# Feed-forward part of a transformer layer: norm applications on ScalarE, attention halves on GpSimd, TensorE's branch ahead of the last value matmul

## The chip, the cores and the metric

The kernel runs on one core of a Trainium2 chip. The core's engines are TensorE (PE: matmuls; PEld: its weight loads), VectorE (DVE), ScalarE (ACT), GpSimd (POOL) and SyncE (SP), which issues the DMAs. Each has its own instruction stream, worked through in program order, and they wait for each other on semaphores. Time is the device time of one execution in microseconds (us).

## The reference

One transformer layer on 4 sequences of 1024 tokens with 256 features, in float32: attention with 16 query heads and 4 key/value heads of width 16, then a gated feed-forward part of width 1024 with integer weights, each with a residual and a layer norm behind it.

```python
def _layernorm(x, axis=-1, eps=1e-05):
    m = jnp.mean(x, axis=axis, keepdims=True)
    v = jnp.var(x, axis=axis, keepdims=True)
    return (x - m) / jnp.sqrt(v + eps)
...
        q = q * cos + _rotate_half(q) * sin
        k = k * cos + _rotate_half(k) * sin
...
        scores = jnp.einsum('bqkgd,bskd->bkgqs', qg, k) * scale
        attn = jax.nn.softmax(scores, axis=-1)
        out = jnp.einsum('bkgqs,bskd->bqkgd', attn, v).reshape(B, S, E)
        return out @ wo
...
        Wg = _dequant(gate_w, gate_scale)   # (w - 128) * scale
        g = jnp.einsum('bsh,ih->bsi', hidden_state, Wg)
        u = jnp.einsum('bsh,ih->bsi', hidden_state, Wu)
        h = jax.nn.silu(g) * u
        return jnp.einsum('bsi,hi->bsh', h, Wd)
...
    x = _layernorm(x + _L0_attn_ref(...), axis=-1)
    x = _layernorm(x + _L0_ffn_ref(...), axis=-1)
```

## The kernel before

The kernel has three parts in time. The projections come first. Then attention runs over 8 pairs of key/value heads, 4 halves for each pair, 8 key tiles `t` for each half. The feed-forward part comes last, over 8 blocks `m` of 512 tokens, from about 768 us of the trace to its end. The change touches the last half of attention and everything behind it.

Matmul operands that need more than the fast format holds are split in two: a high part (`_h`, a cast) and a low part (`_l`, the rest). So nearly every tensor that TensorE reads costs a copy and a subtraction on other engines.

A block `m` of the feed-forward part is this, with `it` from 0 to 7 over slices of 128 of the 1024 hidden features:

- TensorE: `gate_up(it)`, 8 matmuls of 128x512 (L1071), into one of two `pair_bank`s; from `it` 2 on, `down(it-2)`, 8 matmuls of 128x256 (L1080), into `pv_bank` and a ring bank. After `down(3)` come the transposes of the next block's `x1` (L995). After `down(5)` comes the output projection `project_out` of the block after that (24 matmuls, L987), then `down(6)` and `down(7)`.
- ScalarE: `silu(it)` (L893), and behind it, in this order, the high part `hid_h(it-1)` of the hidden slice before (L883). The high part of the transposed `x1` (L847) comes at `it` 5.
- VectorE: `hid(it)` (L758), and between two of them a piece of the work around the block: `y` of the block before (L715, L720), the residual of the next block (L682), its norm statistics (L662, L668, L670), its norm application to `x1` (L675, at `it` 4), the high and low parts of the attention output for the block after that (`bring_attn`: L704, L707, at `it` 4), the second norm of the block before (statistics at `it` 5, application to `y`, also L675, at `it` 7), and the low part of `x1T` (L697, at `it` 5).
- GpSimd: `hid_l(it)` (L528), which `down(it)` waits for, and the two reciprocal square roots (L513, behind `hid_l(2)` and `hid_l(5)`). In block 0 it also scales the last pair's attention output (L509, behind `hid_l(4)`).

So each hidden slice goes PE, ACT, DVE, ACT, POOL and back to PE. The order on each engine is written out by hand. `hid` and `silu` have two buffers each.

TensorE's feed-forward code exists twice, with and without the low parts of the weights. A flag computed from the weights (`use_low`) chooses the copy; TensorE loads it and branches. Before the change this happens right in front of `gate_up(0)` of block 0, behind the last value matmul `pv` (L971) and `project_out(1)`. With these inputs the copy without low parts runs.

## Time and profile before

| what | us |
|---|---|
| median of 3 runs | 1015.37 (1012.94 to 1015.94) |
| the profiled execution, its own time | 1014.48 |
| its span, first to last instruction | 1012.7 |
| TensorE busy | 947.9 |
| VectorE busy | 822.5 |
| ScalarE busy | 696.4 |
| GpSimd busy | 237.3 |

The mean granted clock of TensorE over the span is 0.957 of full speed. In the page's 40 slices of 25.3 us each, the last ten belong to the feed-forward part: TensorE is at 8 or 9 tenths in most of them, VectorE at 6 to 8, ScalarE at 3 or 4 and GpSimd at 2 to 5. A row of the timeline gives the start in us, the duration in us (of all merged instructions together, where it ends in x2 or x4), the engine, the line, the operation, what it writes and reads, and in brackets how long the engine sat idle before it and whom it waited for. Starts and ends of different engines in one trace can be compared.

### The profile page before, as it was taken

The page shows a single profiled execution, that of the slowest core. Times are in us where ns is not written, and L with a number is a line of the kernel's source. Part 1 is how long each engine was busy: PE and PEld are TensorE (multiplying, and loading weights), DVE is VectorE, ACT ScalarE, POOL GpSimd, SP SyncE. Part 2 cuts the span into 40 slices and gives each one's busy share as a digit, 9 for nine tenths or more (in the row PEclk, how much of TensorE's full clock was granted, in tenths as well). Part 3 has the DMA queues.
Part 4 walks back from the last instruction along what each step waited for, and adds up shares of the span by engine and source line. Part 5 has one row for each costly group of instructions (what it writes and reads, how often), then busy time and mean ns, then how long its engine had stood idle before and what let it go on. Part 6 is the DMA issues. An engine that isn't in the chain of part 4 may idle for free.

```text
span 1012.7 us, 15932 instructions
## 1 busy us (share of the span) xinstructions
PE 947.9 (94%) x5632; PEld 475.1 (47%) x5632; DVE 822.5 (81%) x1601; ACT 696.4 (69%) x878; POOL 237.3 (23%) x162
## 2 busy tenths in 40 slices
PE   7886999999999999999999999999997899999985
PEld 3343433333333333333333333333336787777774
DVE  2756689999999999999999999999833678877756
ACT  1324588998999899989989898999983333433332
POOL 9874274000000000000000000000002445544433
PEclk9886589999999999999999999999999999999997
DMA  5667443142232332332323313301201010011001
GB/s 158 207 215 156 146 104 103 33 78 71 52 68 61 73 67 47 83 67 51 79 53 69 68 41 73 87 24 46 73 8 53 21 42 18 25 42 43 22 21 42
DMA packets 48450, 70.65 MB, mean 70 GB/s; under 512 B 15152, under 2 KB 27184, under 8 KB 48368
## 3 DMA queue, kind: packets, MB, share of 16 engines
q1 hardware_dynamic: 47552, 66.45, 26.2%
q0 software_dynamic: 816, 3.15, 1.0%
q8 instruction: 47, 0.77, 0.3%
q14 instruction: 35, 0.29, 0.1%
HBM read 46.47 MB, written 16.25 MB: 62 GB/s over the span
## 4 chain that ended last, share of the span: by engine, by line
PE 66%; DVE 13%; issue 4%; POOL 4%; ACT 4%; POOLq 0%; DVEq 0%; ACTq 0%
PE pv_bank L971 24%; PE ring_bank L948 24%; DVE block_max L607 8%; PE pair_bank L1021 7%; PE pair_bank L1071 6%; POOL hid_l L528 3%; PE pv_bank L1080 2%; ACT probs L867 2%; DVE hid L758 1%; PE ring_bank L1080 1%; DVE x L675 1%; POOL rstd L513 1%; ACT hid_h L883 1%; PE ring_bank L987 1%; ACT silu L893 1%
## 5 line engine op out<-in xcount | busy, mean ns | idle before, releaser
L867 ACT ACTIVATE probs<-pair_bank 128x1024 f32<-128x1024 f32 x512 | 495.6, 1024 | 48.9 <-PE pair_bank L1021 48.9
L607 DVE TENSOR_REDUCE block_max<-ring_bank 128x1 f32<-128x512 f32 x720 | 467.1, 684 | 41.1 <-PE ring_bank L948 30.0
L948 PE MATMUL ring_bank<-k_max,q_sb 64*128 64x512 f32 x1024 | 348.2, 487 | 18.6 <-DMA q_sb<-q_parts 7.8
L948 PEld LDWEIGHTS ring_bank<-k_max,q_sb 64*128 64x128 f32 x1024 | 144.8, 191 | 301.6 <-DVE block_max L607 151.8
L971 PE MATMUL pv_bank<-probs,v_sb 128*32 128x512 f32 x2048 | 273.6, 606 | 1.4 <-ACT probs L867 1.3
L1021 PE MATMUL pair_bank<-q_sb,k_sb 64*128 64x512 f32 x1024 | 251.6, 425 | 1.8 <-ACT probs L867 1.8
L509 POOL TENSOR_TENSOR attn<-attn,inv_rows 128x1024 f32<-128x1024 f32 x8 | 19.5, 2438 | 532.9 <-DMA inv_rows<-inv_d 532.9
L1021 PEld LDWEIGHTS pair_bank<-q_sb,k_sb 64*128 64x128 f32 x1024 | 117.8, 186 | 31.9 <-ACT probs L867 15.7
L893 ACT ACTIVATE silu<-pair_bank,gate_s 128x512 f32<-128x512 f32 x64 | 44.1, 689 | 125.3 <-PE pair_bank L1071 125.2
L528 POOL TENSOR_TENSOR hid_l<-hid,hid_h 128x512 fp32r<-128x512 f32 x64 | 84.7, 1329 | 143.8 <-ACT hid_h L883 143.8
L838 ACT ACTIVATE above<-ring_bank 128x512 f32<-128x512 f32 x152 | 90.6, 598 | 34.5 <-PE ring_bank L948 31.4
L604 DVE CUSTOM_DVE_ANT_0 above<-ring_bank,above 128x512 f32<-128x512 f32 x152 | 103.5, 689 | 12.7 <-ACT above L838 11.3
L758 DVE SCALAR_TENSOR_TENSOR hid<-pair_bank,up_s,silu 128x512 f32<-128x512 f32 x64 | 47.1, 742 | 68.3 <-ACT silu L893 60.1
L971 PEld LDWEIGHTS pv_bank<-probs,v_sb 128*32 128x32 f32 x2048 | 40.3, 108 | 76.0 <-issue 73.3
L811 ACT ACTIVATE high<-rotated 128x512 fp32r<-128x512 f32 (+1 forms) x20 | 12.6, 630 | 64.9 <-POOL rotated L469 64.9
L918 PE MATMUL pair_bank<-x_in,wq_sb 128*128 128x512 f32 x64 | 36.4, 721 | 15.0 <-DMA x_in<-xT 8.2
L1080 PE MATMUL pv_bank<-down_h,hid_h 128*128 128x256 f32 x128 | 37.9, 318 | 12.2 <-POOL hid_l L528 11.5
L1071 PE MATMUL pair_bank<-x1T_h,gate_h 128*128 128x512 f32 x128 | 42.4, 414 | 5.7 <-issue 2.9
L883 ACT ACTIVATE hid_h<-hid 128x512 fp32r<-128x512 f32 x64 | 40.0, 625 | 8.9 <-DVE hid L758 8.7
L1071 PE MATMUL pair_bank<-x1T_l,gate_h 128*128 128x512 f32 x128 | 41.3, 405 | 0.0
L1071 PE MATMUL pair_bank<-x1T_h,up_h 128*128 128x512 f32 x128 | 41.0, 403 | 0.0
L1071 PE MATMUL pair_bank<-x1T_l,up_h 128*128 128x512 f32 x128 | 40.6, 399 | 0.0
(95 smaller groups left out, 879.4 us busy)
## 6 DMA issues: line engine op xcount, KB each, us to landing
q_sb<-q_parts SPq DMA_DIRECT2D x192, 64.0 KB, 2.3
k_max<-k_parts SPq DMA_DIRECT2D x96, 96.0 KB, 3.2
k_sb<-k_parts SPq DMA_DIRECT2D x96, 64.0 KB, 2.4
x_in<-xT SPq DMA_DIRECT2D x8, 512.0 KB, 5.0
q_parts<-high SPq DMA_DIRECT2D x16, 256.0 KB, 4.4
q_parts<-low SPq DMA_DIRECT2D x16, 256.0 KB, 4.7
attn<-pv_sb SPq DMA_DIRECT2D x128, 32.0 KB
inv_rows<-inv_d SPq DMA_DIRECT2D x64, 64.0 KB, 2.3
```

Of the source, the lines that this page charges most:

```text
L528: pool.tensor_tensor(hid_l[:, it, :], hid[it % 2][:], hid_h[:, it, :].bitcast(fp32), ALU.subtract).then_inc(hid_l_ready, 1)
L604: dve.tensor_tensor_reduce(out=buf[:], in0=bank[:], in1=buf[:], scale=1.0, scalar=-3.0e38, op0=ALU.add, op1=ALU.max, accum_out=block_max[h ...
L607: dve.reduce_max(block_max[half % 2][:, col:col + 1], bank[:], axis=AX.X).then_inc(ring_used, 1)
L758: dve.scalar_tensor_tensor(out=hid[it % 2][:], in0=pair_bank[it % 2][:, 1, :], scalar=up_s[:, it:it + 1], in1=silu[it % 2][:], op0=ALU.mul ...
L838: act.activation(above[(count - 1) % 2][:], ring_bank[places[key] % BANKS][:], ACT.Relu).then_inc(above_ready, 1)
L867: act.activation(probs[t % 2][:, 2 * pr:2 * pr + 2, :], pair_bank[pr][:], ACT.Exp, scale=D ** -0.5).then_inc(probs_ready, 1)
L893: act.activation(silu[it % 2][:], pair_bank[it % 2][:, 0, :], ACT.Silu, scale=gate_s[:, it:it + 1]).then_inc(silu_ready, 1)
L948: pe.matmul(bank[:], q_sb[k][rows, i, qt * P:(qt + 1) * P], k_max[k // QH][rows, kind * CH:(kind + 1) * CH], start=True, stop=True).then_i ...
L971: ins = pe.matmul(pv_bank[32 * j:32 * j + 2 * D, :], v_sb[s][:, t, :], probs[t % 2][:, 2 * (j % 2) + j // 2, :], start=(t == 0), stop=(t = ...
L1021: ins = pe.matmul(pair_bank[pr][:, r, :], k_sb[s][rows, t * P:(t + 1) * P], q_sb[k][rows, pr, :], start=True, stop=True)
L1071: ins = pe.matmul(pair_bank[it % 2][:, u, :], w[:, k, it * P:(it + 1) * P], v[c][:, k, :], start=(q == 0), stop=(q == len(terms) - 1))
L1080: ins = pe.matmul(sum_bank[t // 2][:, (t % 2) * E:(t % 2 + 1) * E], v[:, k, t * P:(t + 1) * P], w[:, k, :], start=(k == 0 and t % 2 == 0 a ...
```

## The change

Four things change.

1. Both norm applications go from VectorE to ScalarE. VectorE computed (x - mean) * rstd from two pointers. ScalarE computes rstd * x + offset in one Identity activation. So VectorE also writes `minus_mean` (128x4), and GpSimd multiplies it with rstd into `offset` (128x4) behind each reciprocal square root. For block 0's `x1` ScalarE does it in the last half of attention, behind the exponentials of `t` 3. In the blocks `x1` comes at `it` 4, behind `hid_h(3)`, and `y` at `it` 7, behind `hid_h(6)` and ahead of `hid_h(7)`.
2. `bring_attn` goes from VectorE to GpSimd in two pieces (a cast and a subtraction of 128x512 each), behind `hid_l(0)` and `hid_l(3)`. The halves of blocks 0 and 1 are made early, during attention. The high and low parts of `x1T` move from `it` 5 to `it` 6.
3. TensorE's branch stands ahead of the last `pv`; both copies of its feed-forward code now begin with that `pv` and `project_out(1)`. VectorE computes `use_low` ahead of the low part of `x1T` for block 0. A one-column Silu of a spare tile lets ScalarE load its Silu table ahead of `gate_up(0)`.
4. The space for the early attention halves comes from memory that is used earlier: the weights are split on GpSimd in six pieces of 1024 columns in place of three of 2048, and `pv` reads `v_all` directly, so that the 16 DMAs into `v_sb` and their share of the waits go.

```diff
-                sp.dma_start(v_sb[s][:], v_all[:, 2 * pair + s]).then_inc(kv_loaded[s], 16)
...
+            for n, (w, w_h, w_l) in enumerate(((gate_w, gate_h, gate_l), (up_w, up_h, up_l), (down_w, down_h, down_l))):
                 flat_h, flat_l = (t[:].rearrange("p k n -> p (k n)") for t in (w_h, w_l))
-                pool.tensor_copy(flat_h, w_f[:]).then_inc(w_high, 1)
-                pool.wait_ge(w_high, n + 1)
-                pool.tensor_tensor(flat_l, w_f[:], flat_h.bitcast(fp32), ALU.subtract).then_inc(w_split, 1)
+                rows = w.shape[0] // 2
+                for half in range(2):
+                    i = 2 * n + half
+                    cols = slice(half * I, (half + 1) * I)
...
+            def bring_attn(m, c, k):
+                if m > 1:
+                    pool.wait_ge(wo_ready, 2 * m - 2)
+                src = attn[:, 2 * (m // 2) + k, c * CH:(c + 1) * CH]
+                pool.wait_ge(norm_done, 2 * (m // 2) + 2)
+                pool.tensor_copy(attn_h[c][:, k, :], src).then_inc(attn_h_ready, 1)
+                pool.wait_ge(attn_h_ready, 2 * m + k + 1)
+                pool.tensor_tensor(attn_l[c][:, k, :], src, attn_h[c][:, k, :].bitcast(fp32), ALU.subtract).then_inc(attn_in_ready, 1)
+            def rsqrt(m, ve, r, mm, off, added, done, used, off_done):
+                pool.wait_ge(added, 2 * m + 2)
+                if m:
+                    pool.wait_ge(used, TT * m)
                 pool.tensor_tensor(r[:], ve[:], neg_half[:], ALU.pow).then_inc(done, 1)
+                pool.wait_ge(done, m + 1)
+                pool.tensor_tensor(off[:], mm[:], r[:], ALU.mult).then_inc(off_done, 1)
...
             for pair in range(1, PAIRS - 1):
+                if pair == PAIRS - 2:
+                    for c in range(2):
+                        for k in range(KE):
+                            bring_attn(c, c, k)
                 normalize(pair, False, False)
-            rsqrt(1, var_eps, rstd, eps_added, rstd_ready)
+            rsqrt1(0)
...
                         if it == 2 and not (last and c == 1):
-                            rsqrt(m + 2, var_eps, rstd, eps_added, rstd_ready)
+                            rsqrt1(m + 1)
                         if it == 4 and first and c == 0:
                             normalize(PAIRS - 1, False, True)
+                        if it in (0, 3) and not last:
+                            bring_attn(m + 2, c, it // 3)
                         if it == 5 and not (first and c == 0):
-                            rsqrt(m, var_eps2, rstd2, eps2_added, rstd2_ready)
+                            rsqrt2(m - 1)
             each(B, ffn)
-            rsqrt(2 * B, var_eps2, rstd2, eps2_added, rstd2_ready)
+            rsqrt2(2 * B - 1)
...
                 dve.wait_ge(ready, TT * m + TT)
+                if m:
+                    dve.wait_ge(used, m)
+                dve.tensor_scalar(mm[:], mv[:, :, 0], -1.0, None, ALU.mult).then_inc(added, 1)
                 dve.tensor_scalar(ve[:], mv[:, :, 1], EPS, None, ALU.add).then_inc(added, 1)
-            def apply_norm(m, src, dst, mv, r, ready, done):
-                dve.wait_ge(ready, m + 1)
-                for t in range(TT):
-                    dve.tensor_scalar(dst[:, t, :], src[:, t, :], mv[:, t, 0:1], r[:, t:t + 1], ALU.subtract, ALU.mult).then_inc(done, 1)
...
-                        if it == 4:
-                            if nxt:
-                                if prev:
-                                    dve.wait_ge(sum_ready, m)
-                                norm1_apply(m + 1, 1 - c)
-                            if not last:
-                                bring_attn(b + 1, c)
                         if it == 5:
                             if prev:
                                 norm2_stats(m - 1, 1 - c)
                                 norm2_aggregate(m - 1)
-                            if nxt:
-                                split_x1T(m + 1, 1 - c)
-                        if it == KI - 1 and prev:
-                            norm2_apply(m - 1, 1 - c)
...
+                        if last and k == HALVES - 1 and t == KT - 5:
+                            norm1_apply(0, 0)
...
+            def apply_norm(m, src, dst, r, off, ready, done):
+                act.wait_ge(ready, m + 1)
+                for t in range(TT):
+                    act.activation(dst[:, t, :], src[:, t, :], ACT.Identity, bias=off[:, t:t + 1], scale=r[:, t:t + 1]).then_inc(done, 1)
+            def norm1_apply(m, c):
+                if m > 1:
+                    act.wait_ge(sum_ready, m - 1)
+                apply_norm(m, x_res[c], x1[c], rstd, offset, offset_ready, x1_ready)
+            def norm2_apply(m, c):
+                apply_norm(m, y[c], y[c], rstd2, offset2, offset2_ready, y_ready)
...
+            act.activation(table_carrier[:], neg_half[:, 0:1], ACT.Silu)
...
-                        if it == 5 and not (last and c == 1):
+                        if it == 4 and not (last and c == 1):
+                            norm1_apply(m + 1, 1 - c)
+                        if it == 6 and not (last and c == 1):
                             split_x1T(m + 1, 1 - c)
+                        if it == 7 and not (first and c == 0):
+                            norm2_apply(m - 1, 1 - c)
...
-                    ins = pe.matmul(pv_bank[32 * j:32 * j + 2 * D, :], v_sb[s][:, t, :], probs[t % 2][:, 2 * (j % 2) + j // 2, :],
+                    ins = pe.matmul(pv_bank[32 * j:32 * j + 2 * D, :], v_all[:, head, t, :], probs[t % 2][:, 2 * (j % 2) + j // 2, :],
...
-            pe.wait_ge(probs_ready, 2 * last_g + 2)
-            pv(last_g, HALVES * PAIRS - 1, HALVES - 1, KT - 1, True)
-            project_out(1, 1, False)
-            pe.wait_ge(w_split, 3)
+            pe.wait_ge(w_split, 6)
...
+                pe.wait_ge(probs_ready, 2 * last_g + 2)
+                pv(last_g, HALVES * PAIRS - 1, HALVES - 1, KT - 1, True)
+                project_out(1, 1, False)
                 each(B, ffn)
...
```

TensorE at the branch, before (`use_low` is the flag, `pv_bank` the value matmuls, `ring_bank<-wo_*` is `project_out(1)`, the last row `gate_up(0)`):

```order
L1021 MATMUL pair_bank<-q_sb,k_sb 128x512 x4
L971 MATMUL pv_bank<-probs,v_sb 32x512 x8
L987 MATMUL ring_bank<-wo_h,attn_h 128x256 x2
...
L987 MATMUL ring_bank<-wo_l,attn_h 128x256 x2
L1109 TENSOR_LOAD use_low
L1109 ISA x2
L1110 COMPARE_AND_BRANCH
L1071 MATMUL pair_bank<-x1T_h,gate_h 128x512 x2
```

And after:

```order
L1040 MATMUL pair_bank<-q_sb,k_sb 128x512 x4
L990 MATMUL pv_bank<-probs,v_all 32x512 x4
L1126 TENSOR_LOAD use_low
L1126 ISA x2
L1127 COMPARE_AND_BRANCH
L990 MATMUL pv_bank<-probs,v_all 32x512 x4
L1006 MATMUL ring_bank<-wo_h,attn_h 128x256 x2
...
L1085 MATMUL pair_bank<-x1T_h,gate_h 128x512 x2
```

The load of the flag and the branch moved ahead of the last `pv` and of `project_out(1)`.

ScalarE from `silu(4)` to the end of block 1, before:

```order
L893 ACTIVATE silu<-pair_bank,gate_s 128x512
L883 ACTIVATE hid_h<-hid 128x512
L893 ACTIVATE silu<-pair_bank,gate_s 128x512
L883 ACTIVATE hid_h<-hid 128x512
L847 ACTIVATE x1T_h<-ring_bank 128x512 x2
L893 ACTIVATE silu<-pair_bank,gate_s 128x512
L883 ACTIVATE hid_h<-hid 128x512
L893 ACTIVATE silu<-pair_bank,gate_s 128x512
L883 ACTIVATE hid_h<-hid 128x512 x2
```

And after:

```order
L907 ACTIVATE silu<-pair_bank,gate_s 128x512
L897 ACTIVATE hid_h<-hid 128x512
L878 ACTIVATE x_0<-x_res,offset,rstd 128x256 x4
L907 ACTIVATE silu<-pair_bank,gate_s 128x512
L897 ACTIVATE hid_h<-hid 128x512
L907 ACTIVATE silu<-pair_bank,gate_s 128x512
L897 ACTIVATE hid_h<-hid 128x512
L845 ACTIVATE x1T_h<-ring_bank 128x512 x2
L907 ACTIVATE silu<-pair_bank,gate_s 128x512
L897 ACTIVATE hid_h<-hid 128x512
L878 ACTIVATE v_all<-v_all,offset,rstd 128x256 x4
L897 ACTIVATE hid_h<-hid 128x512
```

Two groups of four 128x256 activations are new; the second (`y`, which lies in `v_all`) stands between `hid_h(6)` and `hid_h(7)`.

GpSimd up to `hid_l(5)` of block 1, before (the first row is `hid_l` 5 to 7 of block 0 and 0 to 2 of block 1):

```order
L528 TENSOR_TENSOR hid_l<-hid,hid_h 128x512 x6
L513 TENSOR_TENSOR rstd<-var_eps,neg_half 128x4
L528 TENSOR_TENSOR hid_l<-hid,hid_h 128x512 x3
```

And after (the first row is `hid_l` 5 to 7 of block 0 and 0 of block 1):

```order
L556 TENSOR_TENSOR hid_l<-hid,hid_h 128x512 x4
L521 CAST attn_h<-attn 128x512
L523 TENSOR_TENSOR attn_l<-attn,attn_h 128x512
L556 TENSOR_TENSOR hid_l<-hid,hid_h 128x512 x2
L529 TENSOR_TENSOR rstd<-var_eps,neg_half 128x4
L531 TENSOR_TENSOR offset<-minus_mean,rstd 128x4
L556 TENSOR_TENSOR hid_l<-hid,hid_h 128x512
L521 CAST attn_h<-attn 128x512
L523 TENSOR_TENSOR attn_l<-attn,attn_h 128x512
L556 TENSOR_TENSOR hid_l<-hid,hid_h 128x512 x2
```

Two casts, two subtractions and the product for `offset` now stand between the `hid_l` that `down` waits for.

## Rows read from the trace of the kernel before

**Rows 1.** Timeline of TensorE (and its weight loads) from the last value matmul.

```profile
760.82 1.06 PE L971 MATMUL pv_bank<-probs,v_sb 128*32 128x512 f32 x8 [1.31 <-ACT probs L867]
...
767.86 0.83 PE L1071 MATMUL pair_bank<-x1T_h,gate_h 128*128 128x512 f32 x2 [2.91 <-issue]
...
791.96 0.99 PE L1071 MATMUL pair_bank<-x1T_h,gate_h 128*128 128x512 f32 x2 [2.01 <-DVE hid L758]
...
800.26 0.28 PE L1080 MATMUL pv_bank<-down_h,hid_h 128*128 128x256 f32 x1
...
865.83 0.36 PE L1080 MATMUL pv_bank<-down_h,hid_h 128*128 128x256 f32 x1 [1.00 <-POOL hid_l L528]
...
868.70 0.28 PE L1080 MATMUL pv_bank<-down_h,hid_h 128*128 128x256 f32 x1
...
874.87 0.38 PE L1080 MATMUL pv_bank<-down_h,hid_h 128*128 128x256 f32 x1 [0.22 <-POOL hid_l L528]
...
887.02 0.19 PEld L1080 LDWEIGHTS pv_bank<-down_h,hid_h 128*128 128x128 f32 x1 [0.28 <-POOL hid_l L528]
...
944.93 0.19 PEld L1080 LDWEIGHTS pv_bank<-down_h,hid_h 128*128 128x128 f32 x1 [0.28 <-POOL hid_l L528]
...
972.67 0.19 PEld L1080 LDWEIGHTS pv_bank<-down_h,hid_h 128*128 128x128 f32 x1 [0.28 <-POOL hid_l L528]
...
1000.57 0.29 PEld L1080 LDWEIGHTS pv_bank<-down_h,hid_h 128*128 128x128 f32 x1 [0.29 <-POOL hid_l L528]
```

**Rows 2.** A 2-us stretch: PE, PEld, DVE, ACT, POOL busy, granted clock, DMA.

```profile
768.00:770.00 2.00, 2.00 (x6) 1.56 (x7) 0.00 (x0) 0.00 (x0) 0.00 (x0) 0.59 0.12 25
```

**Rows 3.** Timeline of VectorE, in block 0 (786.73) and block 3.

```profile
786.73 4.51 DVE L707 TENSOR_TENSOR attn_l<-attn,attn_h 128x512 fp32r<-128x512 f32 x2
...
870.71 0.86 DVE L670 TENSOR_SCALAR var_eps<-mean_var 128x4 f32<-128x4 f32 x1
871.48 1.21 DVE L720 TENSOR_TENSOR v_all<-v_all,x 128x1024 f32<-128x1024 f32 x1
...
873.67 2.27 DVE L675 TENSOR_SCALAR x<-x_res,mean_var,rstd 128x256 f32<-128x256 f32 x4 [0.31 <-POOL rstd L513]
...
884.12 3.32 DVE L675 TENSOR_SCALAR v_all<-v_all,mean_var,rstd 128x256 f32<-128x256 f32 x4
```

**Rows 4.** Timeline of GpSimd in block 3.

```profile
864.41 1.28 POOL L528 TENSOR_TENSOR hid_l<-hid,hid_h 128x512 fp32r<-128x512 f32 x1 [6.36 <-ACT hid_h L883]
...
871.65 1.91 POOL L513 TENSOR_TENSOR rstd<-var_eps,neg_half 128x4 f32<-128x4 f32 x1
873.53 1.29 POOL L528 TENSOR_TENSOR hid_l<-hid,hid_h 128x512 fp32r<-128x512 f32 x1
...
884.35 2.62 POOL L528 TENSOR_TENSOR hid_l<-hid,hid_h 128x512 fp32r<-128x512 f32 x2 [1.57 <-ACT hid_h L883]
```

**Rows 5.** Timeline of ScalarE, last half of attention, first table load, block 3.

```profile
749.20 3.77 ACT L867 ACTIVATE probs<-pair_bank 128x1024 f32<-128x1024 f32 x4 [0.19 <-PE pair_bank L1021]
...
771.34 1.28 ACT L893 ACT_TABLE_LOAD   x1 [8.79 <-PE pair_bank L1071]
...
883.57 1.29 ACT L883 ACTIVATE hid_h<-hid 128x512 fp32r<-128x512 f32 x2 [1.13 <-DVE hid L758]
```

**Rows 6.** Groups by line and shape: count, then busy us, mean ns, idle before.

```profile
L893 ACT ACTIVATE silu<-pair_bank,gate_s 128x512 f32<-128x512 f32 x64 | 44.1, 689 | 125.3 <-PE pair_bank L1071 125.2
L847 ACT ACTIVATE x1T_h<-ring_bank 128x512 fp32r<-128x512 f32 x16 | 8.7, 598 | 5.0 <-PE ring_bank L995 5.0
...
L818 ACT ACTIVATE v_all<-ring_bank 128x256 f32<-128x256 f32 x4 | 1.5, 366 | 0.0
```

**Rows 7.** The same, GpSimd.

```profile
L513 POOL TENSOR_TENSOR rstd<-var_eps,neg_half 128x4 f32<-128x4 f32 x16 | 21.6, 1350 | 35.7 <-DVE var_eps L670 34.5
...
L500 POOL CAST gate_h<-w_f 128x2048 fp32r<-128x2048 f32 x1 | 1.9, 1891 | 0.1
```

**Rows 8.** Timeline of the tail.

```profile
1007.88 1.38 DVE L675 TENSOR_SCALAR v_all<-v_all,mean_var,rstd 128x256 f32<-128x256 f32 x4 [1.12 <-POOL rstd L513]
```

More of the change, by code:

```diff
@@ L109, in layer @@
         rstd = sb("rstd", [P, TT])
+        minus_mean, offset = sb("minus_mean", [P, TT]), sb("offset", [P, TT])
         attn_l = [sb(f"attn_l{c}", [P, KE, CH], f32r) for c in range(2)]
         two = ExitStack()
-        w_raw = sb("w_raw", [P, KE * I], i32, two)
-        w_f = sb("w_f", [P, KE * I], fp32, two)
+        w_raw = sb("w_raw", [P, I], i32, two)
+        w_f = sb("w_f", [P, I], fp32, two)
+        above = [sb(f"above{c}", [P, CH], fp32, two) for c in range(2)]
+        k_max = [sb(f"k_max{s}", [P, S + CH], f32r, two) for s in range(UNITS)]
         q_sb = [sb(f"q_sb{k}", [P, G // GROUPS, CH], f32r, two) for k in range(HALVES)]
-        k_max = [sb(f"k_max{s}", [P, S + CH], f32r, two) for s in range(UNITS)]
         k_sb = [sb(f"k_sb{s}", [P, S], f32r, two) for s in range(UNITS)]
-        v_sb = [sb(f"v_sb{s}", [P, KT, 2 * D], fp32, two) for s in range(UNITS)]
-        above = [sb(f"above{c}", [P, CH], fp32, two) for c in range(2)]
         probs = [sb(f"probs{c}", [P, G, CH], fp32, two) for c in range(2)]
@@ L795, in _ @@
             norm2_aggregate(2 * B - 1)
-            norm2_apply(2 * B - 1, 1)
         @block.scalar
```

66 lines of the change are left out of this document (30 added, 36 removed).

## Prediction

> **What bounds the kernel now.** I looked first at the 40 slices of the page: the feed-forward part is where the change lies, and TensorE is at 8 or 9 tenths there. TensorE sets the pace, so every other engine counts only where TensorE waits for it. Then I read TensorE's timeline for the rows with idle time in front [rows 1]. The blocks follow each other evenly: the last `down(7)` of block 0 starts at 800.26, that of block 5 at 944.93, so blocks 1 to 5 take 28.93 us each. In block 3 TensorE stands still for 1.00 us ahead of `down(0)` (865.83) and for shorter times ahead of `down(3)` (874.87) and `down(7)` (887.02); `down(1)` at 868.70 waits for nothing. All of these waits end with `hid_l` on GpSimd [rows 1]. `down(it)` needs the chain `silu(it+1)`, `hid_h(it)`, `hid_l(it)` behind `gate_up(it+1)`: 0.6 us until `hid_h`, 0.62, and 1.28, with the semaphores about 2.8 us. `down` and `gate_up` of one `it` take 2.87 us together (865.83 to 868.70) [rows 1, 4 to 6]. So the chain just fits, and a microsecond put into it on ScalarE or GpSimd comes out on TensorE.
>
> Three places cost more. In front of `gate_up(0)` of block 0 stands a gap of 2.91 us that the profile gives to nobody (the branch), and the clock behind it is 0.59 [rows 1, 2]. The Silu table is loaded only at 771.34, when the first `silu` is wanted [rows 5]. In block 0 VectorE needs 4.51 us for two subtractions that lie beside GpSimd's work and makes TensorE wait 2.01 us at 791.96 [rows 1, 3].
>
> **Attention.** Without the `v_sb` DMAs nothing ends earlier that TensorE waits for; I count nothing. The six weight pieces on GpSimd have 500 us until they are wanted. The early attention halves lie there too, with nothing behind them that is due.
>
> **The norm application as a price.** The trace has no Identity with two pointers. From below it is bounded by the 128x256 copy out of PSUM, 0.366 us, from above by the 128x512 `silu` with one pointer, 0.689 [rows 6]. One pointer costs 0.689 - 0.598 = 0.09 (`silu` against the copy `x1T_h`, both from PSUM), so two make 0.55 of the copy's 0.366. Two `hid_h` in a row take 1.29, where groups of small ones from PSUM overlap by about 0.1, so I take 0.48 each in a row, 2.0 us for four (bounds 1.5 and 2.8). The Trainium skill (ScalarE: Activation LUTs, What ACT_TABLE_LOAD costs) prices an activation with pointers at 186 ns plus 0.833 ns a column plus 93 ns for each pointer, less 93 ns where they follow each other; that gives an estimate of 0.49 each, and the sum would stay as it is.
>
> **The boundary.** ScalarE runs the exponentials of the last half without a pause: four take 3.77 us from 749.20 [rows 5]. The application for block 0 goes between them, so everything behind comes 2.0 us later. VectorE did it for free. The last value matmuls ran at 760.82, after a gap of 1.31 us, so the `pv` before had ended at 759.5 [rows 1]. Now that end is at 761.5, the branch follows, and with the same gap (2.9 to 3.2 us) the last `pv` starts at about 764.7, 3.9 us later. From there to `gate_up(0)` it was 7.04 us (760.82 to 767.86), of which 3.2 were the branch. That leaves 3.8, plus 1.8 if the half clock that followed the gap now falls on `pv` and `project_out`: `gate_up(0)` starts at 770.3, 2.4 us later than before. Then block 0 runs at full clock from its start. Block 0 took 32.4 us to its `down(7)` (767.86 to 800.26). Out of these go 1.7 for the half clock, 0.8 for the table load (1.28, of which 0.5 was covered by `gate_up(1)`), 2.0 for VectorE and 1.6 for the half clock that I expect behind it, as behind the gap of 2.91. In come 1.1 on GpSimd, where the last pair's scaling now stands behind two added operations and makes `hid_l(5)` late. 27.4 us remain, and `down(7)` of block 0 starts at 797.7: **-2.6 us** (bounds: -4.4 if the clock holds through the new gap, 0 if ScalarE's four applications open a second gap that halves the clock inside attention).
>
> **Blocks 1 to 5, walked in block 3.**
> - `hid_l(0)` ends at 865.69 [rows 4]. The cast takes 1.89/4 = 0.47 [rows 7], the subtraction 1.28 like `hid_l`, with waits 1.9 together. `hid_l(1)` ends at 868.9 and `down(1)` starts at 869.0 instead of 868.70: 0.3 late.
> - At `it` 3 `var_eps` lasted 0.86 us because `hid_l(2)` was running beside it, and the power 1.91 because the 1.21 us of L720 were [rows 3, 4]; alone it is 0.87. So operations of the two engines on SBUF exclude each other in these rows. `minus_mean` adds 0.1 ahead of L720. The product for `offset` is bounded by 0.01 (its share of a 1.28-us subtraction by size) and 0.87 (the power, same shape); I take 0.2, since it is a subtraction's kind of work and not a power. `hid_l(3)` starts at 873.9 instead of 873.53, `down(3)` at 875.3 instead of 874.87: 0.4 late, which takes in the first 0.3.
> - ScalarE applies the norm from 874.0 to 876.0; the transposes want it at 876.2. It just fits. The second attention piece (1.9) and `hid_l(4)` (1.3) fit under `down(3)`, transposes and `gate_up(6)`.
> - VectorE's part is gone: 2.27 + 3.32 and the attention halves. It bought little, since TensorE's waits in these blocks end with GpSimd, and the one on `hid_h` (1.13 us of ScalarE at 883.57, from 882.44) lay beside `project_out`.
> - At the end `silu(7)` comes 0.4 later, `hid_h(6)` follows at once (882.8 to 883.4), then `y` until 885.4, then `hid_h(7)` until 886.0 and `hid_l(7)` until 887.45. `down(7)` starts at 887.5 instead of 887.02.
>
> That is +0.45 a block, **+2.3 us** for five (bounds -1.5 and +8).
>
> The Trainium skill (GPSIMD Reference, section 4.1, Engine selection) says to keep two-input elementwise work on VectorE, since GpSimd takes about twice as long. The rows agree (1.28 us for 512 columns on GpSimd, 1.21 for 1024 in L720 on VectorE). By the rule the move would lose its 1.3 us a block; by the walk above only 0.3 of them reach TensorE, because the rest lies under its matmuls.
>
> **Blocks 6 and 7.** They have no `project_out`, so nothing covers `hid_h(7)` behind `y`. Before, `hid_h(7)` followed `hid_h(6)`, and `down(7)` started at 972.67 and 1000.57 [rows 1]. Now 2.0 us of `y` lie between, of which GpSimd's `hid_l(6)` hides 0.6: +1.4 in each, and +0.2 from `down(3)` in block 6: **+3.0 us**.
>
> **The tail.** Behind the last `down` come the second norm and its application, once 1.38 us on VectorE [rows 8], now 2.0 on ScalarE, with `minus_mean` 0.1 and `offset` 0.3 ahead: **+1.0 us**.
>
> Sum: -2.6 + 2.3 + 3.0 + 1.0 = +3.7. The profiled execution took 1014.48 (its span of 1012.7 and 1.8 around it), so 1018.2 for the like of it; the median of the runs lies 0.9 higher, and I give 1019.0.
>
> **Rivals.**
> - *The cover is larger than I think* (faster). The clock holds at the branch (-1.8), and the blocks get shorter by 0.3 instead of longer, because GpSimd no longer shares SBUF with 8 us of VectorE's work a block, so that `hid` and `hid_l` come earlier (-0.75 x 5 = -3.8 against my sum), and so in block 6 (-0.5). 3.7 - 6.1 = -2.4 to -4: 1012. For it speaks that VectorE is busy in 6 to 8 tenths there and its rows are stretched (2.27, 3.32) [rows 3]; against it that TensorE's waits end elsewhere.
> - *GpSimd's small operations are dear* (slower, much). If the product costs what the power costs, it delays `hid_l(3)` by 0.7 more, and the chain repeats it at `it` 5: +1.4 x 6, +0.7 in the tail, about +9: 1028. For it: no small operation of GpSimd other than the power is timed in this part. It decides from a product of 0.4 us on.
> - *Gain and loss cancel* (no change). An application costs 0.38 in place of 0.48: 0.4 less in each `y`, -0.2 x 5 for the blocks, -0.8 for blocks 6 and 7, -0.4 in the tail: +1.5, 1017.
> - *The change doesn't do what it says*, the gap of the branch is not covered: that is in my sum already (the gap begins 1.3 us earlier in its half and costs the same).
>
> **How the numbers follow.** My forecast, slower by 2 to 6 us: 0.45. Cancelling: 0.25. Faster rival: 0.18. Dear small operations: 0.12. A measurement of this kernel tells 0.3% (3 us) from no change. The forecast case lies above that bound in about 0.37 of its 0.45; so slower 0.37 + 0.12 = 0.49, same 0.33, faster 0.18. The range from 1011.5 to 1025 leaves out the dear rival and the edge of the faster one, 0.18 together; around the likeliest alone it would be 1016.5 to 1022.
>
> **What would show it.** A row of four 128x256 activations of about 2.0 us at `it` 4 and 7; a `hid_h(7)` that starts when `y` ends, and a `down(7)` that waits for `hid_l`; `down(1)` with a wait of 0.3; a last `pv` at about 764.7 and `gate_up(0)` at 770 with full clock; VectorE busy less by about 8 us a block with no shorter block. Wrong would be a period of blocks 1 to 5 below 28.9, a `gate_up(0)` before 768, or applications below 0.4 us.

## The result and the profile after

The changed kernel took 1018.82 us (median of 5 runs, 1016.94 to 1020.36), the kernel before 1013.04 in the runs beside it (5 runs, 1011.89 to 1015.94): a ratio of 1.0047, 95% interval [1.0029, 1.0065], so slower by 0.3 to 0.65%. The profiled execution took 1019.23, its span 1017.4 (before: 1014.48 and 1012.7). VectorE's busy time fell from 822.5 to 761.0 us, ScalarE's rose from 696.4 to 725.2, GpSimd's from 237.3 to 269.4, TensorE's stayed (947.7). In all, 61 us less work on VectorE bought nothing.

I cut the span at the start of `project_out(0)` (741.63 before, 741.14 after) and at the first matmul of each `down(7)`. The numbers are differences of such rows of the two timelines.

| stretch | before | after | difference | forecast |
|---|---|---|---|---|
| start to `project_out(0)` | 741.63 | 741.14 | -0.5 | 0 |
| from there to `down(7)` of block 0 | 58.63 | 57.95 | -0.7 | -2.6 |
| blocks 1 to 5 | 144.67 | 145.90 | +1.2 | +2.3 |
| blocks 6 and 7 | 55.64 | 59.27 | +3.6 | +3.0 |
| from the last `down(7)` to the end | 12.13 | 13.14 | +1.0 | +1.0 |
| sum | | | +4.7 | +3.7 |

TensorE's timeline after, for the rows that answer to [rows 1] (start, duration, engine, line, operation, idle time before and its releaser):

```profile
753.55 0.56 PE L1040 MATMUL pair_bank<-q_sb,k_sb 64*128 64x512 f32 x2 [1.36 <-ACT probs L865]
...
766.31 1.06 PE L990 MATMUL pv_bank<-probs,v_all 128*32 128x512 f32 x8 [3.03 <-issue]
771.78 0.63 PE L1085 MATMUL pair_bank<-x1T_h,gate_h 128*128 128x512 f32 x2
...
799.09 0.28 PE L1094 MATMUL pv_bank<-down_h,hid_h 128*128 128x256 f32 x1
...
865.20 0.36 PE L1094 MATMUL pv_bank<-down_h,hid_h 128*128 128x256 f32 x1 [0.98 <-POOL hid_l L556]
868.27 0.19 PEld L1094 LDWEIGHTS pv_bank<-down_h,hid_h 128*128 128x128 f32 x1 [0.46 <-POOL hid_l L556]
874.59 0.39 PE L1094 MATMUL pv_bank<-down_h,hid_h 128*128 128x256 f32 x1 [0.40 <-POOL hid_l L556]
886.59 0.19 PEld L1094 LDWEIGHTS pv_bank<-down_h,hid_h 128*128 128x128 f32 x1 [0.47 <-POOL hid_l L556]
...
944.99 0.39 PE L1094 MATMUL pv_bank<-down_h,hid_h 128*128 128x256 f32 x1 [0.26 <-POOL hid_l L556]
...
974.48 0.58 PE L1094 MATMUL pv_bank<-down_h,hid_h 128*128 128x256 f32 x1 [0.66 <-POOL hid_l L556]
...
1001.78 0.39 PE L1094 MATMUL pv_bank<-down_h,hid_h 128*128 128x256 f32 x1 [1.76 <-POOL hid_l L556]
1004.26 0.58 PE L1094 MATMUL pv_bank<-down_h,hid_h 128*128 128x256 f32 x1 [1.26 <-POOL hid_l L556]
```

The waits of before stand at the same places with the same releaser; those at `down(7)` of blocks 6 and 7 (974.48, 1004.26) have grown. Two are new: 1.36 us at 753.55, inside attention, behind ScalarE's four applications, and that of the weight load of `down(1)` for `hid_l`, 0.46 us at 868.27, which the forecast named. The wait of 2.01 us in block 0 (791.96) is gone. The gap of the branch is as long as before (3.03, 2.91), only ahead of `pv`.

ScalarE's timeline after, at the boundary, at the end of block 3 and at the end of the kernel [rows 5, 8]:

```profile
750.53 2.06 ACT L878 ACTIVATE x<-x_res,offset,rstd 128x256 f32<-128x256 f32 x4
...
768.05 1.28 ACT L893 ACT_TABLE_LOAD   x1
...
881.99 0.62 ACT L897 ACTIVATE hid_h<-hid 128x512 fp32r<-128x512 f32 x1
882.51 2.08 ACT L878 ACTIVATE v_all<-v_all,offset,rstd 128x256 f32<-128x256 f32 x4
884.50 0.61 ACT L897 ACTIVATE hid_h<-hid 128x512 fp32r<-128x512 f32 x1
...
1011.92 2.07 ACT L878 ACTIVATE v_all<-v_all,offset,rstd 128x256 f32<-128x256 f32 x4 [9.12 <-POOL offset L531]
```

Four applications take 2.06 to 2.08 us. `hid_h(7)` stands behind `y` and starts when it ends. GpSimd in block 3 [rows 4]:

```profile
864.99 0.61 POOL L521 CAST attn_h<-attn 128x512 fp32r<-128x512 f32 x1
865.68 1.29 POOL L523 TENSOR_TENSOR attn_l<-attn,attn_h 128x512 fp32r<-128x512 f32 x1
...
871.10 1.91 POOL L529 TENSOR_TENSOR rstd<-var_eps,neg_half 128x4 f32<-128x4 f32 x1 [0.17 <-DVE var_eps L703]
873.10 0.20 POOL L531 TENSOR_TENSOR offset<-minus_mean,rstd 128x4 f32<-128x4 f32 x1
873.25 1.29 POOL L556 TENSOR_TENSOR hid_l<-hid,hid_h 128x512 fp32r<-128x512 f32 x1
```

The product for `offset` takes 0.20 us, and the power is as long as before, though VectorE has less to do. The granted clock in 2-us stretches of the boundary (the third number from the end; first the stretch, its length and the busy time of PE, PEld, DVE, ACT, POOL), answering to [rows 2]:

```profile
752.00:754.00 2.00, 0.64 (x6) 0.19 (x2) 0.00 (x0) 2.00 (x4) 0.00 (x0) 0.96 0.00 0
754.00:756.00 2.00, 1.65 (x8) 0.49 (x10) 0.00 (x0) 2.00 (x3) 0.00 (x0) 0.50 0.00 0
...
758.00:760.00 2.00, 2.00 (x9) 1.12 (x7) 0.00 (x0) 0.21 (x1) 0.00 (x0) 0.50 0.00 0
760.00:762.00 2.00, 2.00 (x14) 0.57 (x12) 0.00 (x0) 2.00 (x3) 0.00 (x0) 0.83 0.00 0
...
768.00:770.00 2.00, 2.00 (x11) 2.00 (x11) 0.00 (x0) 1.52 (x3) 0.00 (x0) 0.50 0.12 26
```

The clock is at 0.50 of full (1.2 of 2.4 GHz) twice: for 6.8 us behind the 1.36-us gap (753.9 to 760.7), and again for 3.4 us behind the branch.

### The profile page after: what moved, and what is told of

Its sections match the earlier page's. It is cut to its first block, busy times and chain, and to the rows that moved or that the text cites. A ratio compares the mean times of both kernels' runs of the same rounds, so it can differ in the third digit from the quotient of the medians.

```text
span 1017.4 us, 16003 instructions
## 1 busy us (share of the span) xinstructions
PE 947.7 (93%) x5632; PEld 475.4 (47%) x5632; DVE 761.0 (75%) x1521; ACT 725.2 (71%) x943; POOL 269.4 (26%) x222
## 4 chain that ended last, share of the span: by engine, by line
PE 69%; DVE 9%; ACT 6%; POOL 4%; issue 2%; POOLq 0%; ACTq 0%; DVEq 0%
PE pv_bank L990 24%; PE ring_bank L967 24%; PE pair_bank L1085 8%; DVE block_max L637 8%; PE pair_bank L1040 7%; POOL hid_l L556 3%; PE pv_bank L1094 2%; PE ring_bank L1094 2%; ACT probs L865 2%; ACT v_all L878 1%; POOL rstd L529 1%; ACT hid_h L897 1%; PE ring_bank L1006 1%; ACT silu L907 1%; PE ring_bank L1014 1%
## 5 line engine op out<-in xcount | busy, mean ns | idle before, releaser
L865 ACT ACTIVATE probs<-pair_bank 128x1024 f32<-128x1024 f32 x512 | 495.7, 1024 | 51.0 <-PE pair_bank L1040 51.0
L990 PE MATMUL pv_bank<-probs,v_all 128*32 128x512 f32 x2048 | 274.7, 609 | 3.1 <-issue 3.0
L556 POOL TENSOR_TENSOR hid_l<-hid,hid_h 128x512 fp32r<-128x512 f32 x64 | 82.3, 1287 | 124.2 <-ACT hid_h L897 117.4
L990 PEld LDWEIGHTS pv_bank<-probs,v_all 128*32 128x32 f32 x2048 | 40.4, 108 | 78.1 <-issue 77.6
```

The costliest lines, as they stand in the source:

```text
L556: pool.tensor_tensor(hid_l[:, it, :], hid[it % 2][:], hid_h[:, it, :].bitcast(fp32), ALU.subtract).then_inc(hid_l_ready, 1)
L865: act.activation(probs[t % 2][:, 2 * pr:2 * pr + 2, :], pair_bank[pr][:], ACT.Exp, scale=D ** -0.5).then_inc(probs_ready, 1)
L990: ins = pe.matmul(pv_bank[32 * j:32 * j + 2 * D, :], v_all[:, head, t, :], probs[t % 2][:, 2 * (j % 2) + j // 2, :], start=(t == 0), stop= ...
```

## The experiments

All runs are compared with runs of the kernel before on the same chip (medians 1011.74, 1012.06 and 1011.87 us). Ratios are to it, in brackets the 95% interval; 0.001 is 1 us. What a single trace adds is read at the cuts above. Between two traces the time from `project_out(0)` to `down(7)` of block 0 moves by 2 to 3 us through the clock alone, so the blocks are read singly.

| kernel | ratio | `project_out(0)` to `down(7)` of block 0 | mean of blocks 1 to 5 | block 6 | block 7 | tail |
|---|---|---|---|---|---|---|
| before | 1 | 58.63 | 28.93 | 27.74 | 27.90 | 12.13 |
| after | 1.0047 | 57.95 | 29.18 | 29.49 | 29.78 | 13.14 |
| after again | 1.0052 [1.0037, 1.0067] | 55.55 | 29.19 | 29.46 | 29.22 | 13.15 |
| x1 on VectorE | 1.0047 [1.0030, 1.0064] | 54.72 | 29.20 | 29.44 | 29.82 | 13.12 |
| x1 in two parts | 1.0044 [1.0028, 1.0061] | 54.56 | 29.19 | 29.45 | 29.15 | 13.14 |
| branch back | 1.0053 [1.0032, 1.0073] | 54.95 | 29.20 | 29.46 | 27.70 | 12.58 |
| branch alone | 1.0018 [1.0009, 1.0027] | 58.79 | 28.94 | 27.71 | 26.32 | 11.53 |
| y last | 1.0008 [0.9994, 1.0022] | 56.66 | 28.69 | 28.13 | 26.76 | 12.99 |
| halves on VectorE | 1.0070 [1.0058, 1.0083] | 55.37 | 29.41 | 29.19 | 29.13 | 13.11 |
| hid_h first | 0.9901 [0.9886, 0.9916] | 54.53 | 27.12 | 27.40 | 27.47 | 13.04 |
| hid_h first, before | 0.9908 [0.9893, 0.9923] | 55.77 | 28.14 | 26.81 | 24.75 | 11.50 |
| all three | 0.9832 [0.9819, 0.9845] | 53.41 | 26.97 | 26.29 | 24.90 | 12.60 |
| all three, branch back | 0.9845 [0.9830, 0.9860] | 52.70 | 26.97 | 26.30 | 26.43 | 12.61 |
| and tail on VectorE | 0.9830 [0.9813, 0.9847] | 53.31 | 26.97 | 26.29 | 24.89 | 11.62 |

### The boundary

**x1 of block 0 on VectorE.** Off ScalarE's last half of attention, as before the change:

```diff
-                        if last and k == HALVES - 1 and t == KT - 5:
-                            norm1_apply(0, 0)
...
+            dve.wait_ge(rstd_ready, 1)
+            for t in range(TT):
+                dve.tensor_scalar(x1[0][:, t, :], x_res[0][:, t, :], mean_var[:, t, 0:1], rstd[:, t:t + 1], ALU.subtract, ALU.mult).then_inc(x1_ready, 1)
             split_x1T(0, 0)
```

> The changed kernel, with block 0's norm application (x1) back on VectorE; all other applications stay on ScalarE. Theory: in the changed kernel the four activations in the last half of attention cost their own 2.06 us on ScalarE and, through the gap of 1.36 us that they open in front of the scores of t 5, a stretch of half clock worth another 2 to 2.5 us. So gate_up(0) starts 4 to 4.5 us earlier than in the changed kernel (at about 767.5 in place of 771.78), no row between 750 and 760 shows a clock of 0.50, and the median is about 1014.5 (1018.8 less 4.3). Rival: the half clock comes from something else (the transposes or the branch) and only the 2.06 us come back: 1016.8.

Neither size came. The ratio is that of the changed kernel; the 0.8 us by which its boundary is shorter in the traces (54.72 against 55.55 in "after again") is less than the ratios can tell.

**x1 in two parts.** Two applications at `t` 3 and two at `t` 4:

```diff
-                            norm1_apply(0, 0)
+                            act.wait_ge(offset_ready, 1)
+                        if last and k == HALVES - 1 and t in (KT - 5, KT - 4):
+                            for u in (0, 1) if t == KT - 5 else (2, 3):
+                                act.activation(x1[0][:, u, :], ...)
```

> The changed kernel, with block 0's four applications on ScalarE in two pieces: two behind the exponentials of t 3, two behind those of t 4. The same work on the same engine. Theory: TensorE's one gap of 1.36 us becomes two of about 0.6, the clock stays at full through attention, and gate_up(0) starts 2 to 2.5 us earlier than 771.78: about 1016.5. Rival: the half clock follows from the sum of the idle time or from the transposes: no difference, 1018.8.

The gap of 1.36 fell to 0.38 and 0.41, with no gain that the runs can tell: the rival.

**After again.** No edit.

> The changed kernel once more, unchanged, on the chip of these runs. Theory: the half clock behind the 1.36 us gap of the last half of attention (754 to 760 in its first trace), and that in block 7, are not fixed by the program: the gap and the work behind it will be the same, and the clock behind it full, gate_up(0) 27.3 to 29.4 us behind the start of project_out(0) instead of 30.6. Rival: the gap of 1.36 us halves the clock each time, as its first trace had it (30.6).

The theory held. The rows of the second trace of the same program:

```profile
753.26 0.50 PE L1040 MATMUL pair_bank<-q_sb,k_sb 64*128 64x512 f32 x2 [1.36 <-ACT probs L865]
...
763.62 1.48 PE L990 MATMUL pv_bank<-probs,v_all 128*32 128x512 f32 x8 [2.98 <-issue]
```

and its clock:

```profile
754.00:756.00 2.00, 1.82 (x14) 0.75 (x15) 0.00 (x0) 1.95 (x3) 0.00 (x0) 1.00 0.00 0
756.00:758.00 2.00, 2.00 (x19) 0.91 (x17) 0.00 (x0) 0.84 (x1) 0.00 (x0) 1.00 0.00 0
```

The gap is the same, and the clock behind it is full. It was full too, at the same gap, in "branch back", "y last", "halves on VectorE" and "hid_h first". So the half clock inside attention was that one execution's. In this trace the last `pv` starts 22.77 us behind `project_out(0)`; with x1 on VectorE it is 20.78. The applications do delay it by 2.0, as forecast, but `gate_up(0)` follows only 0.9 later (28.25 and 27.39), because from its start `pv` and what follows ran at half clock for 3.4 us in the one and for 5.9 in the other.

**Branch back** (the changed kernel) and **branch alone** (the kernel before). The first moves the last `pv` and `project_out(1)` ahead of the load of the flag again; the second does the opposite to the kernel before, with `use_low` computed early:

```diff
-            pe.wait_ge(probs_ready, 2 * last_g + 2)
-            pv(last_g, HALVES * PAIRS - 1, HALVES - 1, KT - 1, True)
-            project_out(1, 1, False)
...
+                pe.wait_ge(probs_ready, 2 * last_g + 2)
+                pv(last_g, HALVES * PAIRS - 1, HALVES - 1, KT - 1, True)
+                project_out(1, 1, False)
                 each(B, ffn)
```

> The changed kernel, with TensorE's branch where it was before: behind the last value matmul and project_out(1). Theory: the gap of the branch (3.03 us) is the same length at either place, but ahead of the last value matmul 1.3 us of it lie under ScalarE's last exponentials, and the half clock behind it falls on small matmuls instead of gate_up(0). The step is worth 1 to 2 us: 1020.3. Rival: the branch ahead of pv is worth nothing or costs (its half clock is the same in length): 1018.8 or below.

> The kernel before the change, with one part of the change alone: the flag's load and the branch ahead of the last value matmul (and use_low ahead of the low part of x1T). Theory: the branch costs its 2.9 us wherever it stands, and the 1.31 us that TensorE waited for probs in front of the last pv is hidden under it, so the stretch from project_out(0) to gate_up(0) gets shorter by about 1 us, and block 0 keeps its 32.4 us less what half clock there is behind the gap: 0 to -2 us against the kernel before, ratio 0.998 to 1.000. Rival: the branch is the cause of the whole half clock at the boundary and block 0's clock is worth what I counted (-1.7): -3 us or more, ratio 0.997 or below.

Branch back: no difference, the rival. In its trace the gap of the branch is 2.31 us and the clock behind it stays full. Branch alone: both expectations fell, it is 1.8 us slower. With the branch ahead the gap was 3.29 and `pv`, `project_out` and the first matmuls ran at half clock from 766 to 772; before, the gap was 2.91 behind 1.31 us of waiting. What `pv` no longer waits, the clock takes back: 58.79 against 58.63 us in these two traces. That explains why nothing was gained, and not the 1.8 us: this trace is longer by 3.4 us in its first 61 us, ahead of everything that the edit touches. Where the 1.8 us stand is open.

### The blocks

**y last.** The second norm's application behind `hid_h(7)`:

```diff
-                        if it == 7 and not (first and c == 0):
-                            norm2_apply(m - 1, 1 - c)
                     hid_high(KI * m + KI - 1, KI - 1)
+                    if not (first and c == 0):
+                        norm2_apply(m - 1, 1 - c)
```

> The changed kernel, with the application to y behind hid_h(7) in place of ahead of it. Theory: y delays hid_h(7) by 2.06 us, which blocks 6 and 7 pay nearly in full (29.49 and 29.78 us in the changed kernel, 27.74 and 27.90 before) and blocks 1 to 5 by some tenths. So blocks 6 and 7 fall to about 27.9 each, blocks 1 to 5 to about 29.0, together -4.5 us: 1014.3. Rival: down(7) then waits for something nearly as late (GpSimd's queue, the power for the second norm), or y comes too late for the output and the next block: -1 us or nothing, 1018.

The theory held: 3.9 us by the ratios. Each of blocks 1 to 5 is 0.5 shorter and block 6 1.36. Of the 3.0 in block 7 about 2 are clock, since "branch back", with `y` ahead of `hid_h(7)` but no half clock there, takes 27.70. That this comes and goes for the same code is seen in the kernel before and in "branch alone" behind the same wait for `hid_l` (1.57 and 1.55 us in block 6), one row of each:

```profile
974.00:976.00 2.00, 2.00 (x7) 1.61 (x7) 0.00 (x0) 0.00 (x0) 0.00 (x0) 0.50 0.78 262
```

```profile
978.00:980.00 2.00, 2.00 (x10) 1.63 (x9) 0.00 (x0) 0.25 (x1) 0.00 (x0) 1.00 0.77 262
```

Their blocks 7 take 27.90 and 26.32 us.

Blocks 1 to 5 are now 0.24 shorter than in the kernel before (28.69 against 28.93), so the work taken off VectorE was worth something. In block 3, `down(7)` follows `down(6)` after 0.96 us without a wait, where it was 1.29 (28.68 - 27.72 and 28.92 - 27.63 in the table below). Before, ScalarE waited 1.13 us for `hid` ahead of `hid_h(6)` [rows 5]; now it waits 0.29, ahead of `hid_h(7)`, and `hid_l(6)` starts 0.7 us earlier in the block:

```profile
881.39 0.63 ACT L897 ACTIVATE hid_h<-hid 128x512 fp32r<-128x512 f32 x1 [0.29 <-DVE hid L766]
```

**Halves on VectorE.** In the blocks `bring_attn` goes back to VectorE at `it` 4:

```diff
-                        if it in (0, 3) and not last:
-                            bring_attn(m + 2, c, it // 3)
...
+                        if it == 4 and not last:
+                            bring_attn(b + 1, c)
```

> The changed kernel with the blocks' attention halves back on VectorE at it 4 (those of blocks 0 and 1 still made early). Theory, from the walk of block 3: GpSimd's pieces cost 0.3 us a block at down(1), and VectorE has room without the norm applications, so blocks 1 to 5 come down from 29.2 to about 28.9 us (-1.5 in all); in block 0 the two subtractions lie beside the scaling of the last pair again and TensorE waits there up to 2 us. In all -1.5 to +0.5 us against the changed kernel, ratio to before 1.003 to 1.005. Rival: taking the halves off VectorE is what kept the blocks as short as they are: blocks 1 to 5 at 29.5 us or more, ratio 1.007 or above.

The theory fell, the rival's sign is right: 29.41 a block against 29.18, 2.3 parts in a thousand slower in all. The starts in block 3, in us behind `down(7)` of block 2, each read from one row of the timeline:

| start of | before | after | halves on VectorE | y last | hid_h first | hid_h first, before |
|---|---|---|---|---|---|---|
| `down(0)` | 7.73 | 7.81 | 7.82 | 7.70 | 6.92 | 6.88 |
| `down(1)` | 10.60 | 10.88 | 10.71 | 10.79 | 10.01 | 9.74 |
| `down(3)` | 16.77 | 17.20 | 17.44 | 17.11 | 15.75 | 15.33 |
| transposes | 17.89 | 18.25 | 18.50 | 18.16 | 16.70 | 17.34 |
| `down(6)` | 27.63 | 27.82 | 28.08 | 27.72 | 26.11 | 26.74 |
| `down(7)` | 28.92 | 29.20 | 29.44 | 28.68 | 27.13 | 28.11 |

GpSimd's first piece costs 0.17 at `down(1)`, of the 0.3 in the walk. But VectorE's halves cost more at `down(3)`:

```profile
869.21 2.08 POOL L529 TENSOR_TENSOR rstd<-var_eps,neg_half 128x4 f32<-128x4 f32 x1 [0.17 <-DVE var_eps L701]
...
870.84 0.75 DVE L727 CAST attn_h<-attn 128x512 fp32r<-128x512 f32 x2
871.37 0.27 POOL L531 TENSOR_TENSOR offset<-minus_mean,rstd 128x4 f32<-128x4 f32 x1
871.60 1.27 POOL L556 TENSOR_TENSOR hid_l<-hid,hid_h 128x512 fp32r<-128x512 f32 x1
```

With VectorE's cast beside them, the power takes 2.08 in place of 1.91 and the product 0.27 in place of 0.20, and both stand ahead of `hid_l(3)`. The kernel before had no such meeting: there the halves stood behind the norm application, which waited for the power [rows 3]:

```profile
875.86 0.75 DVE L704 CAST attn_h<-attn 128x512 fp32r<-128x512 f32 x2
```

So this run prices halves on VectorE right behind `hid(3)`. Halves on VectorE that wait for the power as before were not run with the norm on ScalarE.

**hid_h first.** ScalarE makes `hid_h(it-1)` ahead of `silu(it)` and no longer behind it; once in the changed kernel, once in the kernel before:

```diff
                         n = KI * m + it
+                        if it:
+                            hid_high(n - 1, it - 1)
                         act.wait_ge(gu_ready, n + 1)
...
-                        if it:
-                            hid_high(n - 1, it - 1)
-                        elif not (first and c == 0):
+                        if it == 0 and not (first and c == 0):
                             act.wait_ge(down_ready, 2 * m)
```

> The changed kernel with one order on ScalarE changed: hid_h(it-1) is issued ahead of silu(it) and no longer behind it. Theory: every wait of down on hid_l in the blocks (0.98 at down(0), 0.46 at down(1), 0.84 at down(3), 0.5 at down(7)) is length of the chain silu, hid_h, hid_l behind gate_up, and hid_h has to wait 0.69 us for a silu that it doesn't need; ahead of it, hid_h comes about 2 us earlier: blocks 1 to 5 come down from 29.2 to 27.0 to 27.7 us, in all -10 to -14 us against the changed kernel, ratio to before 0.991 to 0.995. The wait at down(7) behind y stays. Rival: GpSimd's own work (hid_l, the attention pieces, the power) sets these waits; then only the part of hid_h goes, -0.3 us a block or nothing, ratio 1.002 to 1.005.

> The kernel before the change with the one order on ScalarE changed: hid_h(it-1) ahead of silu(it). Theory: the waits of TensorE in the blocks came from the order on ScalarE and have nothing to do with the change, so the kernel before gains as much by it as the changed one did (which went from 1.0047 to 0.9901 of the kernel before, 14.8 us), and since y stands on VectorE and keeps hid_h(7) free, nothing is left over at down(7): ratio 0.984 to 0.988, blocks of 27.0 us. Rival: VectorE, which has 8 us more work in each block, then sets the pace (hid late behind the attention halves and the norm at it 4), and the blocks stay at 28 us: ratio 0.990 to 0.994, and the change is what makes the order pay.

In the changed kernel the theory held, with a little more than its 10 to 14 us: 14.8 us less, blocks of 27.12, and no wait ahead of a matmul in TensorE's rows of block 3. ScalarE's rows there:

```profile
862.86 0.64 ACT L897 ACTIVATE hid_h<-hid 128x512 fp32r<-128x512 f32 x1 [0.82 <-DVE hid L766]
864.48 0.69 ACT L909 ACTIVATE silu<-pair_bank,gate_s 128x512 f32<-128x512 f32 x1 [0.98 <-PE pair_bank L1085]
```

`hid_h` starts when `hid` is ready and is done before `gate_up` lets the next `silu` go. Behind `silu` it had no such wait: it came late. In the kernel before, the theory's size fell and the rival held. The blocks stop at 28.14, and TensorE waits for VectorE now:

```profile
871.22 1.09 PE L995 MATMUL ring_bank<-ident,x 128*128 128x128 f32 x8 [0.89 <-DVE x L675]
...
881.99 0.39 PE L1080 MATMUL pv_bank<-down_h,hid_h 128*128 128x256 f32 x1 [0.26 <-POOL hid_l L528]
```

With this order the norm on ScalarE and the halves on GpSimd are worth 1.0 us a block (28.14 to 27.12). The two ratios are alike all the same, since blocks 6 and 7 (+0.6 and +2.7, `y` ahead of `hid_h(7)` and the clock) and the tail (+1.5, of which 0.5 is clock) take it back.

**All three**, then with **branch back**, then with the last `y` **on VectorE**:

```diff
             norm2_aggregate(2 * B - 1)
+            dve.wait_ge(rstd2_ready, 2 * B)
+            for t in range(TT):
+                dve.tensor_scalar(y[1][:, t, :], y[1][:, t, :], mean_var2[:, t, 0:1], rstd2[:, t:t + 1], ALU.subtract, ALU.mult).then_inc(y_ready, 1)
...
-            norm2_apply(2 * B - 1, 1)
```

> The changed kernel with three edits together: x1 of block 0 on VectorE, y applied behind hid_h(7), and hid_h(it-1) ahead of silu(it). Theory: the three places are apart, so their gains add: about -2 for the first, -7 for the second, -10 to -14 for the third, in all 998 to 1001 us, ratio to before 0.986 to 0.990. Rival: y in front of hid_h(7) and the order of hid_h and silu cost the same waits, so that the second and third overlap: no better than the third alone by more than 2 us.

> The best version so far (x1 of block 0 on VectorE, y behind hid_h(7), hid_h ahead of silu; 0.9832 of the kernel before) with TensorE's branch back behind the last value matmul. Theory: the branch costs 2.3 to 3.3 us wherever it stands, and which stretch runs at half the clock behind it differs from one execution to the next more than the place does: within 1 us of the same kernel with the branch ahead, ratio 0.982 to 0.985. Rival: ahead of the last pv the gap brings 6 us of half clock onto pv, project_out and gate_up, and behind it less, so that it is 2 us or more faster with the branch back, ratio 0.981 or below.

> The same as the kernel e9b of this call with one application more on VectorE: the last block's y, behind which only the DMA out stands (GpSimd still computes the product, which nothing then waits for). Theory: the term of the tail was 2.0 for 1.38 us of application and 0.2 to 0.3 for the product: -0.9 to -1.0 us in the tail, 12.6 down to 11.6 us from the last down(7) to the end. Rival: the tail is set by the DMA out and the clock, and less than 0.3 of it comes back.

The three together take 995.76 us (5 runs, 994.98 to 995.83), 1.7% less than the kernel before. Against hid_h first alone that is 7 us, where the theory had 9 for the other two edits and the rival allowed 2: in the traces 1.1 of them lie in the boundary and block 0, 0.8 in blocks 1 to 5, 1.1 in block 6 and 2.6 in block 7, where a stretch at half clock is gone too. The ratio is below the range given, but that range doesn't follow from its own terms: they add to 19 to 23 us off the changed kernel, and 21.8 (1.0047 to 0.9832) came off. The branch's place makes no difference that can be told: 995.76 again. In the tail, 12.61 became 11.62:

```profile
988.02 1.01 POOL L529 TENSOR_TENSOR rstd<-var_eps,neg_half 128x4 f32<-128x4 f32 x1 [5.79 <-DVE var_eps L703]
989.06 1.38 DVE L800 TENSOR_SCALAR v_all<-v_all,mean_var,rstd 128x256 f32<-128x256 f32 x4 [1.12 <-POOL rstd L529]
```

That is the 1.0 us of the tail's term, in the trace; the medians (995.49 and 995.76) don't resolve it. This version and "all three" are the best ones found.

## Why the prediction was right

The mechanism and the sum held: slower, 1018.8 where 1019.0 was given, +4.7 in the profiled execution where the sum was +3.7. That it came so close is partly luck. Three terms missed in both directions. And the forecast was set on the 1015.37 of three runs of the kernel before; with the two runs made beside the changed kernel their median is 1013.04, so between the medians the change cost 5.8 us (5.1 in "after again", 1016.98 against 1011.87), where the forecast had 3.7.

- **What bounds.** Every wait of TensorE in the blocks still ends with `hid_l`, and taking 61 us off VectorE made no block shorter than before in the changed kernel. That it "bought little" held: 0.24 a block, seen once `y` was out of the way. The reason given was wrong in part, since the wait of 1.13 us for `hid` [rows 5], put down as lying beside `project_out`, did reach `down(7)`, by the rows of "y last". "A microsecond put into the chain on ScalarE or GpSimd comes out on TensorE" was right, and stronger than I used it: taken out of the chain it comes out too (hid_h first, -2.06 a block).
- **The application's price.** 2.06 to 2.08 for four, taken 2.0. One alone is 0.59 (the mean of the 64), so they start 0.49 apart (3 x 0.49 + 0.59 = 2.06). By the prediction's estimate from the Trainium skill (ScalarE: Activation LUTs, What ACT_TABLE_LOAD costs) an application in a row takes 0.49, and the trace agrees.
- **The product, the power, the cast.** 0.20, as taken, so "dear small operations" is out. The power takes 1.01 where nothing of VectorE lies beside it (0.87 was taken); no term of the sum hung on that. The cast took 0.61 where 0.47 was scaled from the 2048-column one [rows 7].
- **The boundary, -2.6.** The steps: last `pv` 23.1 us behind `project_out(0)` by the forecast (764.7 - 741.63), 22.7 to 23.1 in four traces of the same boundary code; `gate_up(0)` 28.7, and 28.2 to 29.3 in those four; from there to `down(7)` of block 0 27.4, measured 27.31. The 27.4 is right as a sum only: up to `down(0)` the half clock and the table load were put at 2.5 and gave 1.8, and the 1.1 for a late `hid_l(5)` was about 0.1 (`down(4)` to `down(5)` takes 3.0 us in block 0 and 2.9 in block 3). The profiled execution itself fell on the bound that the term named, a second half clock inside attention (25.2, 30.6), and kept 0.7 of the 2.6. In the second trace it is -3.1.
- **Blocks 1 to 5, +0.45 each; measured +0.25.** `down(1)` +0.28 (0.3 forecast), `down(3)` +0.43 (0.4). The late part was right and the end too dear: the lateness shrinks to 0.19 until `down(6)`, and the wait of the weight load at `down(7)`, now set by `y`, is 0.47 where it was 0.28. If the parts add, they are by the runs: `y` ahead of `hid_h(7)` +0.50, the halves on GpSimd -0.23, the rest 0. So the halves cost in my walk and gain in the run: I counted what GpSimd's pieces delay, and not what VectorE's halves delay. Part of that comes from where the run put them, beside the power, and against halves placed as before the sign is open. By the rule of the Trainium skill that I weighed (GPSIMD Engine Reference, section 4.1, two-input work stays on VectorE) the move would have lost. In block 3 GpSimd is indeed the slower one, 1.29 us for a subtraction against 0.90 on VectorE (1.80 for the two with the halves there) and 0.61 against 0.38 for a cast; the blocks are shorter with the halves on GpSimd all the same.
- **Blocks 6 and 7, +3.0; measured +3.6.** Without half clock in block 7, 26.32 (branch alone) stands against 27.70 (branch back): +1.38, the 1.4 of the text. Block 6 has +1.75 (forecast 1.6). The other 0.5 is clock: in "after again" the stretch at half clock in block 7 is as long as in the kernel before (3.4 us, 6.8 in the first trace), and there the two blocks have +3.0.
- **The tail, +1.0.** Measured +1.01, and -0.99 when undone. The tail varies by 0.6 with the clock of the last `down(7)`; of the traces where that is full, branch back has 12.58 and branch alone 11.53, +1.05.
- **The rivals.** The faster one had something right: with VectorE relieved `hid` does come earlier, and "y last" shows it (-0.24 a block). But `y` ahead of `hid_h(7)` took more than that, and the clock did not hold behind the branch. That the branch's gap isn't covered was in the sum, and both runs of it show that moving the branch ahead gains nothing that can be told.

Open: why the same gap is followed by half a clock in one execution and by a full one in the next, and the 1.8 us of "branch alone". The -0.5 us ahead of `project_out(0)` tells nothing: there the traces of kernels with the same code differ by 2.1 us (740.85 to 742.94). Removing the gap of the branch itself was not tried.
